# Per-row scalars in place of second tensor inputs: gamma, the difference's bias and GpSimd's scaling in a fused differential-attention block

## The reference

```python
x = x + 0.5 * ffn(layernorm(x))      # expert choice: each of 16 experts takes its 256 best tokens
x = x + attn(layernorm(x))
x = x + 0.5 * ffn(layernorm(x))
```

```python
s_a  = softmax(causal(q_a @ k_a.T / sqrt(D)))           # a = 0, 1
diff = softmax(causal(s_0 - lam[head] * s_1))
att  = rmsnorm(diff @ v) * rms_w * (1 - LAM_INIT)
```

## Time and profile before

| | |
|---|---|
| time, median of 3 runs | 1824.33 us (1821.73 to 1828.74) |
| profiled execution, its own time | 1832.2 us |
| its span | 1830.4 us |
| mean granted TensorE clock | 0.869 |
| busy: TensorE, VectorE, ScalarE, GpSimd | 1465.6, 1454.8, 1261.2, 1084.6 us |
| bytes moved by transfers | 115.99 MB, mean 63 GB/s |

### The profile page before, as it was taken

One profiled execution on the slowest core, in us unless ns is written; L12 is line 12 of the kernel. 1 busy time (PEld: TensorE's weight loads), 2 busy tenths in 40 slices (PEclk: granted clock), 3 DMA queues, 4 the chain that ended last, 5 costly groups with the idle time before them and its releaser, 6 DMA issues. The chain is left out here.

```text
span 1830.4 us, 43823 instructions
## 1 busy us (share of the span) xinstructions
PE 1465.6 (80%) x10688; PEld 1028.4 (56%) x10688; DVE 1454.8 (79%) x5505; ACT 1261.2 (69%) x3426; POOL 1084.6 (59%) x1493
## 2 busy tenths in 40 slices
PE   3996735988889898988888988888888888888620
PEld 3542313766666666666666666666666666566310
DVE  6778416888898888889988888888989877684477
ACT  2362325787788788878888888878878777675320
POOL 5421534666677777777777777777767666554300
PEclk9998866788899999989999999899989977886855
DMA  8024221111111111111111111111111100001186
GB/s 305 2 64 151 83 68 32 35 36 32 30 46 45 50 44 50 44 44 47 48 44 44 44 44 44 44 44 50 49 45 50 47 22 17 17 23 41 41 314 251
DMA packets 178954, 115.99 MB, mean 63 GB/s; under 512 B 139090, under 2 KB 139474, under 8 KB 178899
## 3 DMA queue, kind: packets, MB, share of 16 engines
q1 hardware_dynamic: 178898, 115.34, 21.4%
HBM read 50.26 MB, written 33.55 MB: 46 GB/s over the span
## 5 line engine op out<-in xcount | busy, mean ns | idle before, releaser
L1670 ACT ACTIVATE ex<-bank,nbias 128x512 f32<-128x512 f32 (+3 forms) x1024 | 528.8, 540 | 80.9 <-DVE bank L1214 78.6
L1214 DVE TENSOR_SCALAR_CACHE_REDUCE bank<-bank,nesc 128x512 f32<-128x512 f32 (+3 forms) x1024 | 503.2, 551 | 88.8 <-PE bank L1925 88.1
L1955 PEld LDWEIGHTS bank<-vs,pr 128*128 128x128 f32 x2560 | 332.8, 205 | 24.3 <-issue 12.3
L1955 PE MATMUL bank<-vs,pr 128*128 (+1 forms) x2560 | 337.6, 283 | 10.2 <-DVE att L1260 5.7
L1937 PE MATMUL bank<-cst,df 128*128 128x128 f32 x1280 | 264.6, 309 | 85.9 <-ACT pr L1687 85.2
L1923 PE MATMUL bank<-ks,hall 96*128 (+2 forms) x1024 | 266.7, 337 | 71.5 <-ACT ex L1670 48.1
L1517 POOL TENSOR_SCALAR ex<-ex,gam 128x128 f32<-128x128 f32 (+3 forms) x512 | 318.7, 635 | 0.0
L1687 ACT ACTIVATE pr<-bank 128x128 f32<-128x128 f32 (+3 forms) x512 | 232.3, 454 | 87.9 <-PE bank L1937 86.8
L1240 DVE CUSTOM_DVE_ANT_0 df<-ex 128x128 f32<-128x128 f32 (+3 forms) x512 | 261.3, 525 | 8.5 <-issue 4.0
L1937 PEld LDWEIGHTS bank<-cst,df 128*128 128x128 f32 x1280 | 168.4, 166 | 114.4 <-ACT pr L1687 99.0
L1670 ACT ACTIVATION_READ_ACCUMULATOR ex<-bank,nbias 128x1 f32 x1024 | 223.8, 219 | 0.0
(11 more groups left out here) (358 smaller groups left out, 2942.1 us busy)
## 6 DMA issues: line engine op xcount, KB each, us to landing
hall<-turned SPq DMA_DIRECT2D x360, 64.0 KB, 2.1
x_dram<-hall SPq DMA_DIRECT2D x8, 1024.0 KB, 4.9
hall<-x_dram SPq DMA_DIRECT2D x8, 1024.0 KB, 14.5
c_y<-y_dram SPq DMA_DIRECT2D x8, 1024.0 KB, 14.5
out_dram<-hall SPq DMA_DIRECT2D x8, 1024.0 KB, 4.7
hall<-in_x SPq DMA_DIRECT2D x7, 1024.0 KB, 13.8
x<-x_dram SPq DMA_DIRECT2D x28, 256.0 KB, 2.7
x_dram<-x SPq DMA_DIRECT2D x28, 256.0 KB, 2.0
```

Source lines behind the costliest of these rows:

```text
L1214: dve.tensor_scalar(part, part, nesc[:, 0:1], None, ALU.mult, ALU.min, accum_out=nbias[:, j, i, a:a + 1]).then_inc(bias_done.sem, 1)
L1670: ac.activation(ex[j % 4][:, a, lo:hi], energy(j, i)[:, a, :], ACT.Exp, bias=nbias[:, j, i, a:a + 1], scale=-1.0, accum_out=esum[:, j, i, ...
L1955: mm = pe.matmul(bank[:, 7, t * DV:(t + 1) * DV], pr[j % 2][:, lo + k * P:lo + (k + 1) * P], val, start=(k == 0), stop=(k == t))
```

## The change

Three instructions get other operands, one pair changes its order, and one wait gets another signal:

- `gamma` becomes lam * r_1, by an operation with one tensor input and one per-row scalar. The factor sum_0 moves to GpSimd's scaling, which takes two per-row scalars, sum_0 and gamma, in place of gamma and the constant 1.
- `diff_bias` computes only the long tile's value (128x1), with r_0 as a per-row scalar and -1 as a constant. The short tile's value isn't formed: GpSimd's shift computes (df - dmax) * r_0 in place of df * r_0 + bias, and so waits for the short difference itself.
- On VectorE `diff_bias` stands ahead of `gamma` in slot 1.

```diff
@@ gamma
-                    dve.scalar_tensor_tensor(out=gam[:, j, :], in0=esum[:, j, :, 0], scalar=lam[:, ds(h, 1)],
-                                             in1=rsum[:, j, :, 1], op0=ALU.mult, op1=ALU.mult)\
+                    dve.tensor_scalar(gam[:, j, :], rsum[:, j, :, 1], lam[:, ds(h, 1)], None, ALU.mult)\
                        .then_inc(gam_done.sem, 1)
@@ diff_bias
-                    dve.scalar_tensor_tensor(out=dbias[:, j, :], in0=dmax[:, j, :], scalar=-1.0,
-                                             in1=rsum[:, j, :, 0], op0=ALU.mult, op1=ALU.mult)\
+                    dve.tensor_scalar(dbias[:, j, 1:2], dmax[:, j, 1:2], rsum[:, j, 1, 0:1], -1.0, ALU.mult, ALU.mult)\
                        .then_inc(dbias_done.sem, 1)
@@ VectorE's order
-                            [(1, inv_sums), (1, gamma), (4, diff_bias), (3, difference(0))],
+                            [(1, inv_sums), (4, diff_bias), (1, gamma), (3, difference(0))],
@@ GpSimd: scale
-                        gp.tensor_scalar(ex[j % 4][:, 1, lo:hi], ex[j % 4][:, 1, lo:hi], gam[:, j, i:i + 1], 1.0,
-                                         ALU.mult, ALU.mult).then_inc(scaled.sem, 1)
+                        gp.tensor_scalar(ex[j % 4][:, 1, lo:hi], ex[j % 4][:, 1, lo:hi], esum[:, j, i, 0:1],
+                                         gam[:, j, i:i + 1], ALU.mult, ALU.mult).then_inc(scaled.sem, 1)
@@ GpSimd: shift
-                    dbias_done.wait(gp, at.units(1), apart_p)
+                    diff_done.wait(gp, at.units(2, 0), apart_p)
                     lo, hi = span(j, 0)
-                    gp.tensor_scalar(df[j % 4][:, lo:hi], df[j % 4][:, lo:hi], rsum[:, j, 0, 0:1],
-                                     dbias[:, j, 0:1], ALU.mult, ALU.add).then_inc(shifted_short.sem, 1)
+                    gp.tensor_scalar(df[j % 4][:, lo:hi], df[j % 4][:, lo:hi], dmax[:, j, 0:1], rsum[:, j, 0, 0:1],
+                                     ALU.subtract, ALU.mult).then_inc(shifted_short.sem, 1)
```

## The result

The changed kernel takes 1861.03 us (median of 4 runs, 1858.21 to 1864.00) against 1823.88 us of the kernel before: a ratio of 1.020 (95% interval 1.0171 to 1.023), or 37 us slower. The forecast was 1813 us, with a range up to 1836.

What follows compares the result with a forecast made beforehand. VectorE paces full bodies at 2.4 GHz, TensorE the rest. VectorE's -26 - 6 + 5 = -27 us, times 0.41 arriving, gives 11 us off 1824.3: 1813 us, range 1792 to 1836.

Steps and rivals of the forecast that it cites:

- steps 1 and 2: On VectorE: two-element gamma keeps its 57 us of GpSimd waits, one-element bias escapes, its 33 us move to short difference.
- step 3: On VectorE: the bias's place behind gamma is gained, 26 us, and some 6 us of the short differences' waits go.
- keep its own: On VectorE: the long difference keeps its own excess of waiting for GpSimd, so no change was priced for it.
- step 4: GpSimd's scaling: second pointer adds 0.07 us each, 36 us of GpSimd time, and 5 us to VectorE's waits.
- GpSimd has room: Claim on GpSimd's scaling: GpSimd is busy only 31 to 34 of 41 to 46 us per full body.
- step 5: GpSimd's shift waits for the short difference, not the bias: 38.7 us of GpSimd idle goes, net VectorE effect zero.
- GpSimd becomes late: Rival, chance 0.18: the scaling's 36 us delay GpSimd's queue and the lower halves; 1849 us passed whole, 1831 by half.
- TensorE's clock took nothing back: Clock rival, chance 0.27: a denser TensorE may be granted a lower clock; 1824 us, between 1817 and 1831.

Runs made afterwards that it cites:

- the addition ahead: Kernel before with GpSimd's first rotary addition of a body issued one slot earlier, ahead of a mask and two scalings: 1804.70 us, ratio 0.9873.

## Why the prediction was wrong, step by step

- **Gamma goes on waiting, the bias escapes, the wait passes to the short difference (steps 1 and 2): right.** 418 ns with a longest of 1251; 172 to 214 ns, with a median of 181 where 0.21 to 0.22 us were forecast from an int32 line; the short forms' means up by 190 and 76 ns, which makes 34 us where 33 were said to move. VectorE's idle time ahead of gamma fell from 33.7 to 16.1 us, which agrees with the bias's place being hidden there. For gamma the trace agrees with the rule that the prediction quotes from the Trainium skill (SBUF — State Buffer, "Who interferes with whom"), by which a tensor_scalar can contend: the 128x2 form still waited, up to 1251 ns. That a single element escapes is told by the rows alone.
- **VectorE's saving (step 3): not seen in the time by itself.** Two biases ahead of gamma, with nothing added on GpSimd, gave 0.9987 (0.9951 to 1.0023); 11 us would be 0.994, which the interval leaves out. That kernel has one bias instruction more than the forecast's. With the addition ahead the same step made a body at 1.00 0.3 us shorter (41.5 to 41.2), 7 us in 22 bodies, and the median fell by 7.7 us, within intervals that overlap. The long difference didn't "keep its own": 15 us more in the changed kernel.
- **The second pointer (step 4): 0.07 us each as said, at every size, but its price was taken at some 5 us of VectorE's waits under "GpSimd has room".** Alone, with the one-input gamma, it costs 0.42% (8 us). The room, 10 to 12 us per body, isn't where the queue is: in the stretch shown there is no gap from the root to the rotary addition.
- **The shift (step 5) is the step that failed.** I priced its wait, its place and its neighbours, and took its duration, "0.45 to 0.55 us", over from the row of a multiply and add to a subtract and multiply. It took 0.79 and 1.21: 115 us more of GpSimd (159.0 + 103.4 against 86.7 + 61.0 us by the same view of the kernel before). The prediction put this difference at nothing without a row for it: no row of GpSimd in the trace before showed a subtraction with a per-row scalar, and the instruction's name was the same. The runs showed in its place that this one term costs 1.1% (0.77 to 1.49) put alone into the kernel before, and 1.2 to 1.5% beside the rest of the change: more than the forecast's whole gain of 11 us. One sign was there to see: the first stage's normalisation on GpSimd (L725) adds a negated mean, for which VectorE spends an instruction (L596).
- **The rival "GpSimd becomes late" was right in kind.** It put the wait at the lower halves for TensorE, and priced 36 us passed whole at 1849. That wait grew too, but little (weight load 22.3 to 31.3 us); the larger one showed one queue further, at ScalarE's, and the surplus was 162 us instead of 36. TensorE's clock took nothing back in the changed kernel: it rose, 0.869 to 0.882 in the mean. Between the kernels with the addition ahead it did matter: TensorE's busy time in the 22 bodies differs there by 23 to 33 us.

How the 37 us split is settled for the causes: the subtraction 1.1% alone and 1.2 to 1.5% with the rest of the change, the second pointer 0.4 to 0.6%, the order nothing that shows. Of the ways to the end, ScalarE's queue is shown (its wait grew, and moving the addition took it away with 39 us of TensorE's idle time in the 22 bodies). VectorE's waits and the granted clock were each seen to differ; how much either carries stays open.

## What to carry to other kernels

Take an instruction's price from a row with the same engine, operands and arithmetic; the form's name and shape aren't enough, and in this program a subtraction on GpSimd is worth turning into an addition of a negated scalar. An engine busy 59% of the time can still have a stretch without a gap with another engine at its end: look for it before adding half a microsecond per step, and try the order there first. Then compare bodies at the same granted clock before calling a gain by its cause: here a moved addition gave 1.3% in one kernel and nothing in another with 0.5 us more of GpSimd per step, since the clock moved too. A wait for shared access that is taken out of one instruction passes to the next one that needs it.

## What the runs showed of the hardware

- GpSimd's TENSOR_SCALAR with a subtraction, first or second, takes 0.79 us for 128 and 1.21 for 256 float32 elements, with additions and multiplications 0.44 and 0.55.
- A second per-row pointer in place of a constant costs GpSimd's scaling 70 ns: shortest 367 to 437 for 128 elements, 687 to 757 for 512.
- A one-element TENSOR_SCALAR of VectorE never waited for GpSimd in 512 executions beside a GpSimd busy 62% of the time (193 to 216 ns); one of two elements took up to 1.25 us, against 0.22 undisturbed.
- GpSimd's power doesn't keep VectorE out, though it reads SBUF: in the kernel before 54 gammas and biases with two tensor inputs lie inside the 28 powers of 2.9 us, and none took over 222 ns. One place of the timeline:

```profile
887.65 2.92 POOL L1627 TENSOR_TENSOR ast<-ast,half 128x16 f32<-128x16 f32 x1 [2.05 <-DVE ast L1367]
...
889.75 0.22 DVE L1228 SCALAR_TENSOR_TENSOR gam<-esum,lam,rsum 128x2 f32<-128x2 f32 x1 [0.24 <-DVE rsum L1221]
```

- Executions of one kernel differ by 25 us together with TensorE's granted clock: two biases ahead of gamma took 1814 us at a mean clock of 0.877 and 1840 at 0.862.
